# Loads of SyncE paced by gather landings, and sixteen unread products ahead of the user part

## The reference

```python
retrieved = jnp.mean(item_embeddings[indices], axis=1)
fused_input = jnp.concatenate([user_rep, retrieved], axis=1)
fused_rep = fused_input @ W_fuse + b_fuse
logits = fused_rep @ W_proj + b_proj
```

## Time and profile before

| | |
|---|---|
| time, median of 3 runs | 305.21 us (304.99 to 305.96) |
| the profiled execution's own time | 304.82 us |
| its span, first to last instruction | 303.0 us |
| granted TensorE clock, mean | 1.000 |
| busy: PE, PEld, DVE, ACT, POOL | 290.6, 236.1, 242.4, 159.8, 73.1 us |
| DMA moved | 75.14 MB, mean 248 GB/s |

### The profile page before, as it was taken

One profiled execution on the slowest core, in us unless ns is written; L12 is line 12 of the kernel. 1 busy time (PEld: TensorE's weight loads), 2 busy tenths in 40 slices (PEclk: granted clock), 3 DMA queues, 4 the chain that ended last, 5 costly groups with the idle time before them and its releaser, 6 DMA issues.

```text
span 303.0 us, 4031 instructions
## 1 busy us (share of the span) xinstructions
PE 290.6 (96%) x1351; PEld 236.1 (78%) x1351; DVE 242.4 (80%) x355; ACT 159.8 (53%) x217; POOL 73.1 (24%) x76
## 2 busy tenths in 40 slices
PE   3996999999999999999999999999999999999995
PEld 1446887888888888888778888888888888888884
DVE  5897999668667789769998979979799797995133
ACT  3005665544544558968465685556845568453310
POOL 4785786777777100000000000000000000000000
PEclk9999999999999999999999999999999999999999
DMA  7999999896997247558875939749397493443315
GB/s 259 359 390 297 406 382 379 301 369 240 313 384 267 78 136 212 184 163 323 280 280 180 352 130 296 284 153 351 136 291 284 153 364 129 144 154 115 130 70 203
DMA packets 32480, 75.14 MB, mean 248 GB/s; under 512 B 4445, under 2 KB 20587, under 8 KB 32460
## 3 DMA queue, kind: packets, MB, share of 16 engines
q1 hardware_dynamic: 25340, 58.31, 54.6%
q0 software_dynamic: 5536, 13.73, 13.2%
q10 hardware_dynamic: 1584, 2.84, 2.5%
HBM read 52.84 MB, written 25.60 MB: 259 GB/s over the span
## 4 chain that ended last, share of the span: by engine, by line
PE 48%; DVE 3%; issue 1%; ACT 0%; DVEq 0%; ACTq 0%
PE pair L1273 16%; PE pair L1275 16%; PE pair L1276 16%; DVE w_lo L977 1%; DVE part_out L1002 0%; DVE out_sb L1002 0%; DVE t_sums L960 0%; DVE w_raw L968 0%; ACT odd_sum L653 0%; DVE out_sb L1135 0%; DVE t_sums L966 0%; DVE t_sums L972 0%; DVEq L998 0%; DVEq L971 0%; ACTq L648 0%
## 5 line engine op out<-in xcount | busy, mean ns | idle before, releaser
L446 POOL DMA_INDIRECT ring<-item_embeddings,rows x56 | 59.0, 1053 | 19.6 <-issue 13.7
L1273 PE MATMUL pair<-w_hi,s_hi 128*128 128x500 f32 x144 | 56.1, 390 | 0.5 <-ACT odd_sum L653 0.3
L1275 PE MATMUL pair<-w_lo,s_hi 128*128 128x500 f32 x144 | 56.0, 389 | 0.0
L1276 PE MATMUL pair<-w_hi,s_lo 128*128 128x500 f32 x144 | 55.8, 388 | 0.0
L1199 PE MATMUL pair<-w_hi,f_hi 128*128 128x500 f32 x112 | 44.3, 395 | 0.0
L1199 PE MATMUL pair<-w_lo,f_hi 128*128 128x500 f32 x112 | 43.8, 391 | 0.0
L869 DVE SCALAR_TENSOR_TENSOR pair<-ring,mask,pair 128x512 f32<-128x512 f32 x48 | 36.2, 754 | 9.4 <-DMA ring<-item_embeddings,rows 5.2
L1199 PE MATMUL pair<-w_hi,f_lo 128*128 128x500 f32 x112 | 43.5, 389 | 0.0
L1275 PE MATMUL pair<-w_lo,f_hi 128*128 128x500 f32 x108 | 42.0, 389 | 0.0
L1276 PE MATMUL pair<-w_hi,f_lo 128*128 128x500 f32 x108 | 41.9, 388 | 0.0
L1273 PE MATMUL pair<-w_hi,f_hi 128*128 128x500 f32 x108 | 41.8, 387 | 0.0
(11 more groups left out here) (142 smaller groups left out, 425.1 us busy)
## 6 DMA issues: line engine op xcount, KB each, us to landing
w_raw<-w_proj SPq DMA_DIRECT2D x28, 500.0 KB, 7.7
logits<-part_out SPq DMA_DIRECT2D x24, 500.0 KB, 3.2
early<-w_proj SPq DMA_DIRECT2D x22, 500.0 KB, 5.7
logits<-out_sb SPq DMA_DIRECT2D x23, 250.0 KB, 2.5
logits<-out_sb SPq DMA_DIRECT2D x11, 500.0 KB, 3.2
first_bias<-b_proj SPq DMA_DIRECT2D x10, 250.0 KB, 7.1
s_sum<-b_proj SPq DMA_DIRECT2D x8, 250.0 KB, 6.6
logits<-out_sb ACTq DMA_DIRECT2D x7, 250.0 KB, 7.2
```

Source lines behind the costliest of these rows:

```text
L446: return nc.gpsimd.indirect_dma_start(out=to, out_offset=None, in_=table, in_offset=bass.IndirectOffsetOnAxis(ap=column, axis=0), **how)
L1273: nc.tensor.matmul(ps[:, q, 0:CHUNK], f, hi, start=start and k == 0, stop=False, skip_group_check=True)
L1275: nc.tensor.matmul(ps[:, q, 0:CHUNK], f, lo, start=False, stop=False, skip_group_check=True)
L1276: m = nc.tensor.matmul(ps[:, q, 0:CHUNK], f_rest, hi, start=False, stop=stop and k == 1, skip_group_check=True)
```

## The change

It has four parts. VectorE sets 256 columns of a not yet used piece of `w_hi` to 1, and TensorE runs 16 products on it ahead of `user_part(0)`, into a bank that is overwritten later; nobody reads them. ScalarE issues only quarters 0 and 1 of user_t; SyncE issues quarters 2 and 3. SyncE's loads wait for gathers of tile 0 to land, each for one slot (`behind_slot`), and `wf_ret` now goes ahead of chunk 1. And VectorE's wait for `bias_lo_ready` stands behind the load of the lap count in `add_home(0)` instead of ahead of it.

```diff
+WARM = 16
+USER_BEHIND = (0, 2)
...
+        warm = w_hi[:, 2 * UNITS - 1, :, :].rearrange("p k n -> p (k n)")
...
-            def load_chunk(c):
-                for h in range(2):
+            def load_chunk(c, halves=(0, 1)):
+                for h in halves:
...
+            def behind_slot(i):
+                sp.wait_ge(slot_landed[place(0, i)], 16 * slot_uses(0, i))
+
             for k in range(HK):
+                if k >= HK // 2:
+                    behind_slot(USER_BEHIND[k - HK // 2])
+                    sp.dma_start(user_t[:, k, :], user_dram[k]).then_inc(user_landed[k], 16)
                 sp.dma_start(wf_user[:, k, :], wf_dram[0, :, k, :]).then_inc(wf_user_landed[k], 16)
                 if k == 0:
                     sp.dma_start(idx[:, K:TILES * K], indices[:, K:TILES * K]).then_inc(idx_landed, 16)
+            behind_slot(3)
+            load_chunk(0, (0,))
+            behind_slot(4)
             sp.dma_start(last_rows[:], last_item.to_broadcast([P, H])).then_inc(last_landed, 16)
-            load_chunk(0)
             sp.wait_ge(total_zeroed, 1)
...
             sp.dma_start(bf_col[:], b_fuse).then_inc(bf_landed, 16)
+            behind_slot(5)
+            load_chunk(0, (1,))
+            behind_slot(6)
+            sp.dma_start(wf_ret[:], wf_dram[1]).then_inc(wf_ret_landed, 16)
+            behind_slot(8)
             load_chunk(1)
-            sp.dma_start(wf_ret[:], wf_dram[1]).then_inc(wf_ret_landed, 16)
             sp.wait_ge(user_fused, 1)
-            sp.wait_ge(slot_landed[place(0, GATE)], 16 * slot_uses(0, GATE))
+            behind_slot(GATE)
...
-            for k in range(HK):
+            for k in range(HK // 2):
                 act.dma_start(user_t[:, k, :], user_dram[k]).then_inc(user_landed[k], 16)
...
                 if t == 0:
                     dve.wait_ge(last_added, 1)
+                    dve.wait_ge(bias_lo_ready, 1)
...
+            nc.vector.memset(warm[:, 0:2 * P].bitcast(F32), 1.0).then_inc(warm_ready, 1)
             number()
...
             bias_lo()
-            dve.wait_ge(bias_lo_ready, 1)
             dve.wait_ge(laps_ready, 2)
             add_home(0)
...
+            pe.wait_ge(warm_ready, 1)
+            for x in range(WARM):
+                nc.tensor.matmul(total_ps[:, 0:2 * P], warm[:, 0:P], warm[:, 0:2 * P], start=True, stop=True)
             user_part(0)
```

More of the change, by code:

```diff
@@ L159, in retrieval_scores @@
         a_ps = pairs_ps[2:4]
+        warm_ready = sem("warm_ready")
         first_idx_landed = sem("first_idx_landed")
```

## The result

The changed kernel takes 312.97 us (median of four runs, 310.68 to 315.19), beside 305.45 for the kernel before on the same chip: a ratio of 1.0245, with a 95% interval of 1.0169 to 1.0321. The execution that was profiled is the fastest of the four: 310.68 us, a span of 308.8 us, a mean granted clock of 0.989 (before: 304.82, 303.0 and 1.000). The other three had a mean clock of 0.984, 0.984 and 0.978.

A forecast was written before the change was run, and what follows sets the result against it. The prediction took VectorE's chain to the home add, then mean(0), to set the projection's start at 35.23 us. +3.5 + 2.1 - 0.3 = +5.3 on 304.82 gave 310.1, and a median of about 310.5 us; range 306.0 to 313.4.

The forecast's parts named there:

- the sum's 310.1: Forecast time of the profiled execution: +3.5, +2.1 and -0.3, so +5.3 us on 304.82.
- Warm products, 0: TensorE's start: unread products cost 0; the 2.06 us saved from the cold start goes nowhere, as TensorE waits for VectorE.
- The wait for bias_lo, 0.76 and covered: VectorE before the home add: moving the wait saves 0.76 us, covered by the later mean(0).
- User pairs 2 and 3: user_t quarters on SyncE: last lands at about 17, allowed until 18.8; cost 0, or 1 us if 1 us later than allowed.
- The paced loads, +3.5: SyncE's queue: lost DMA time lands chunk 1 at 33.0 instead of 21.9, so mean(0) starts 3.5 us later.
- the late bound: Chunk 1's landing at 35.5 if SyncE gets no more than half throughout and gather 0 takes 4 us.
- The gathers land sooner: Start of tile 0: gather 0 lands 3.3 us after issue instead of 7.9, the queue being nearly empty.
- TensorE's clock, +2.1 before fuse(0): TensorE idles some 4.7 us before fuse(0), falls to the half clock and loses 2.1 us.
- Chunk 6, -0.3: VectorE's idle of 0.42 us at 52.18 for chunk 6 goes, giving back 0.3 us.
- worse: Rival: chunks 2 to 4 late too, chunk 1 landing at 35.5, mean(0) +6.0, clock lost, 313.3 us; chance 0.04.

The follow-up runs named there:

- e6: The changed kernel without its sixteen unread warm products: 312.33 us, ratio 1.0216 to the kernel before.
- e1: The kernel before with only VectorE's wait for bias_lo_ready moved behind the register load in add_home(0): 305.78 us, ratio 0.9994.
- e10: The changed kernel with share_last and mean(0) ahead of chunk 1's splits on ScalarE: 311.09 us, ratio 1.0168 to the kernel before.
- e12: The changed kernel with last_rows read from 128 different table rows instead of the last row 128 times: 312.58 us, ratio 1.0240 to the kernel before.
- e4: The changed kernel with 14 unread products ahead of slot 9's sum and 6 behind the sums: 311.57, 312.58 and 315.19 us, ratio 1.0195 to the kernel before.
- e5: The changed kernel with last_rows loaded in the first, unpaced batch: 311.53 us, ratio 1.0169 to the kernel before.
- e2: The changed kernel with chunk 0, last_rows, chunk 1 and wf_ret unpaced in the earlier order, user pairs still paced: 310.88 us, ratio 1.0166 to the kernel before.
- e7: The kernel before with a single wait, for the gather in slot 0, ahead of last_rows on SyncE: 306.88 us, ratio 1.0046.
- e11: The kernel before with chunk 1 behind wf_ret and behind slot 8, nothing paced ahead of it: 305.87 us, ratio 0.9986.
- e9: The kernel before with eight unread products of 500 columns in TensorE's gap before slot 9, bias_lo wait not moved: 304.50 us, ratio 0.9950.
- e8: The kernel before with the bias_lo wait moved and eight unread products of 500 columns in TensorE's gap before slot 9: 304.91 us, ratio 0.9969.

## Why the prediction was right or wrong

The direction, the place and the mechanism were right: SyncE's loads lose DMA time, chunk 1 is the last of them, it stands ahead of mean(0) on ScalarE, and the projection starts late by as much. 312.97 lies in the range, toward its end, and the profiled execution's 310.68 is near the sum's 310.1. But two terms were off and cancelled there (+6.46 for +3.5, nothing for +2.1), so that nearness is luck.

- *Warm products, 0*: right (e6).
- *The wait for bias_lo, 0.76 and covered*: right in size (0.85 in e1) and in being covered. What covers it is more than I said: the lap's gather is late too (28.75), and already in the kernel before the gather in slot 9 left only some 0.3 us of it to gain (e1).
- *User pairs 2 and 3*: sized too low. The last one starts to be multiplied at 19.85, TensorE waits 2.07 for it, and the packing follows at 23.36 instead of 22.27. It is 1 us late, the bound I gave; that cost is hidden behind chunk 1.
- *The paced loads, +3.5*: this is the step that failed, in size: it is **+6.46**. The 0.80 MB lost at 5.5 to 9.5 came out exactly, and the 0.3 after it as 0.40. From 14.19 on SyncE's queue was indeed not empty; what failed is the full 0.39 MB per us that I took from this. The engines moved 279 GB/s from 14.5 to 23: 0.94 MB less, or 2.4 us more. Chunk 1's second half landed at 36.1, not 33.0, and beyond the late bound of 35.5. From there to mean(0) it is 1.6 us, 1.7 in the forecast.
- *The gathers land sooner*: gather 0 does (3.5 us after its issue in place of 7.9), the later ones do not. Slots 9 and 10 land 2.7 and 2.6 us later than before, which I had left out of the sum: the sums end at 36.29, not 30.4. It shows in e10, where they, not chunk 1, set mean(0).
- *TensorE's clock, +2.1 before fuse(0)*: right that the clock is lost, wrong in its place in the profiled run. The clock fell in the gap before slot 9, and the half clock lay under ScalarE's longer wait, at no cost. Where the sums were over early, it fell as forecast: the passes of fuse(0) take 5.18 (e6), 5.26 (e12), 6.36 (e4) and 6.61 us (e5) for 3.81. The Trainium skill, "TensorE: Matmul & The Clock Gate", section "Why this matters for your kernels", says that idle gaps between bursts lose the clock; the trace agrees, at the earlier gap (3.37 us idle, then 0.50), and a gap of 1.94 us lost it in e1. That the three longer runs, at a clock of 0.984 and 0.978, paid it before fuse(0) is argued: they have no trace.
- *Chunk 6, -0.3*: right (0.42 gone).

Of the rivals, "worse" came nearest, with its landing at 35.5 and 313.3, though not by chunks 2 to 4: TensorE is busy for all of 41 to 51 us. I gave it 0.04, because I took the count of bytes for exact and only the shares of the queues for uncertain.

## What to carry to other kernels

Where transfers saturate the DMA engines later on, the bytes that they do not move early are paid by the transfer that comes last, whichever that is (chunk 1, wf_ret in e2, a gather in e7; e11 loses few early bytes and pays nothing): leave such loads unpaced and set only their order. When counting what a pause costs, count its recovery too: it was about as much again here. And a wait of some 2 us of TensorE between bursts can be worth filling with unread products where the fill ends about when the wait does (the sums follow it at 27.10 in e9, and started at 27.00 before); it was the only gain found (-0.3% in e8, -0.5% in e9).

## What the runs showed of the hardware

**After a pause in one queue the DMA engines move less for a while, and look busy.** Queues of the change, 14.5 to 23 us, then of the kernel before in the same stretch (packets, MB, share of 16 engines):

```profile
q1 hardware_dynamic: 700, 1.36, 57.9%
q0 software_dynamic: 311, 1.01, 37.6%
```

```profile
q0 software_dynamic: 529, 1.70, 53.0%
q1 hardware_dynamic: 681, 1.59, 49.7%
```

A share of 37.6% of 16 engines over 8.5 us is 51.1 us for 311 packets of the gathers, 0.164 each, at 3.2 KB; before it is 0.136 at the same size. SyncE's packets take 0.112 at 1.94 KB, before 0.099 at 2.33 KB. So the share of 0.96 hides longer packets. Of the bytes that are missing, 0.69 MB are the gathers' and 0.23 SyncE's, though GpSimd issues its gathers at the same pace (five and the lap's in either stretch). Why the packets are longer is open: the last row's address does not explain it (e12), its load as a whole at most 31 of the 110 GB/s (e5). Nor does it take loads that are issued one by one: in e7 the low rate lasted 4 us although 1.29 MB were waiting, and in e2, where SyncE issues 1.81 MB from 13.84 to 16.3, 200 GB/s move from 17.5 to 19.5 at a share of 0.77.

**The clock falls in some executions and not in others, for the same program.** The kernel before had its gap of 2.4 us at full clock in the profiled run, but the mean clocks of its 22 runs beside e9 fall into two groups, 0.998 and over and 0.992 to 0.994. One trace at 1.000 said nothing of how near the fall was.
